# Row statistics of 35 tiles of the second layer norm: from VectorE to a router column and a ScalarE accumulator

## The reference, cut to what matters

```
xn = layernorm(x)
x  = x + graph_attention(xn, src, dst) + linear_attention(xn)
x  = x + experts(layernorm(x))

# in experts(x):
logits = x @ Wr + br                       # 256 -> 8
top_p, top_idx = top_k(softmax(logits), 2)
mu  = x.mean(-1);  var = ((x - mu)**2).mean(-1)
xn  = (x - mu) * rsqrt(var + 1e-5)
# each token goes through the FFNs (256 -> 1024 -> 256) of its two experts,
# weighted by the two renormalised probabilities
```

## Time and profile before

| | |
|---|---|
| median of three runs | 1897.31 us |
| profiled execution, first to last instruction | 1890.1 us |
| around it, against the median of the runs | 7.2 us |
| edge walk | some 95 to 1198 us |
| steps with late work | some 1012 to 1194 us |
| from the walk to the first FFN matmuls | to some 1285 us |
| mean granted TensorE clock | 0.937 |

### The profile page before, as it was taken

How to read it: one execution, slowest core, us unless ns; L and a number is a source line. 1 busy time by engine, 2 the same in 40 slices (tenths; PEclk the granted TensorE clock), 3 DMA queues, 4 the chain that set the end, 5 groups by cost and what they waited for, 6 DMA issues and landing times. The chain is left out here.

```text
span 1890.1 us, 46784 instructions
## 1 busy us (share of the span) xinstructions
PE 1581.7 (84%) x11358; PEld 1300.0 (69%) x11358; DVE 1368.5 (72%) x3833; ACT 1079.1 (57%) x3043; POOL 1218.3 (64%) x1135
## 2 busy tenths in 40 slices
PE   7858777788787989888887778629999999999995
PEld 5635555455566777777775666517888889888884
DVE  6656567677667888888888999897666656665662
ACT  4655566566666666677666776563444444444441
POOL 2077777777777777777677776105666666666663
PEclk8978899999999999999998888658999999999998
DMA  7745565566544555555555665652333333333332
GB/s 223 247 122 138 168 174 164 165 176 179 150 117 127 155 150 150 141 152 145 142 139 179 183 202 162 200 199 45 53 48 53 49 48 50 53 50 49 46 53 24
DMA packets 149158, 239.37 MB, mean 127 GB/s; under 512 B 27536, under 2 KB 114824, under 8 KB 147624
## 3 DMA queue, kind: packets, MB, share of 16 engines
q0 software_dynamic: 61216, 132.39, 30.4%
q1 hardware_dynamic: 85944, 103.15, 16.8%
q10 hardware_dynamic: 1744, 0.85, 0.2%
HBM read 180.78 MB, written 55.52 MB: 125 GB/s over the span
## 5 line engine op out<-in xcount | busy, mean ns | idle before, releaser
L843 POOL DMA_INDIRECT w_s<-table,w_s x784 | 806.4, 1029 | 279.9 <-issue 231.4
L2092 PE MATMUL bank<-w_s 128*128 128x260 f32 x1952 | 515.9, 410 | 110.3 <-DVE w_s L1536 110.0
L2092 PEld LDWEIGHTS bank<-w_s 128*128 128x128 f32 x1952 | 378.1, 201 | 206.0 <-DVE w_s L1536 139.9
L1026 ACT ACTIVATE w_s<-w_s 128x64 f32 x976 | 260.3, 337 | 68.3 <-ACT w_s L1021 68.1
L1536 DVE SCALAR_TENSOR_TENSOR w_s<-w_s 128x256 f32<-128x256 f32 x732 | 275.7, 426 | 26.7 <-ACT w_s L1026 18.9
L2294 PE MATMUL bank<-acc,w_s 128*128 128x256 f16 (+1 forms) x2736 | 290.4, 265 | 1.6 <-DVE acc L1937 1.5
L2315 PE MATMUL bank<-w_s,acc 128*128 x2520 | 284.5, 273 | 7.2 <-DVE acc L1951 5.5
L907 POOL DMA_INDIRECT out<-mid_g,low_g x105 | 177.2, 1687 | 151.2 <-ACT mid_g L1197 90.6
L2294 PEld LDWEIGHTS bank<-acc,w_s 128*128 x2736 | 252.9, 98 | 30.7 <-issue 2.1
L2315 PEld LDWEIGHTS bank<-w_s,acc 128*128 128x128 f16 x2520 | 245.8, 98 | 37.0 <-issue 8.7
L1033 ACT COPY w_s<-bank 128x512 bf16<-128x512 bf16 x244 | 142.1, 582 | 202.8 <-PE bank L2072 202.3
(11 more groups left out here) (308 smaller groups left out, 2187.6 us busy)
## 6 DMA issues: line engine op xcount, KB each, us to landing
stage<-in_L_ffn_W SPq DMA_DIRECT2D x32, 512.0 KB, 4.2
w_s<-table,w_s POOLq DMA_INDIRECT x784
w_s<-in_x SPq DMA_DIRECT2D x48, 256.0 KB, 4.0
w_s<-xT_d SPq DMA_DIRECT2D x96, 128.0 KB
w_park<-low_g SPq DMA_DIRECT2D x18, 512.0 KB
w_s<-w_park SPq DMA_DIRECT2D x9, 1024.0 KB, 9.1
xn_d<-acc SPq DMA_DIRECT2D x7, 896.0 KB, 5.0
table<-w_s SPq DMA_DIRECT2D x24, 260.0 KB, 3.5
```

What stands on the lines that cost most here:

```text
L843: pool.indirect_dma_start(out=ring[:, u, k, :], out_offset=None, in_=table[:, :], in_offset=bass.IndirectOffsetOnAxis(ap=srcT[:, (q * RING ...
L1026: last = act.activation(m[:, e, 0:GD], rows[:, e, 0:GD], ACT.Copy, scale=m[:, e, GD:HC])
L2092: last = pe.matmul(bank[2 + k.at % 2][:, 0:ROW], hot32[:, k.at % 4, s, :], msg[:, k.at % 2, s, :], start=s == 0, stop=s == SUB - 1)
```

## The change

Tiles 0 to 34 get their statistics in another way. The router matrix in the main memory gets a ninth column with the constant 1/256; it isn't centred, and the product with a raw row is that row's mean. ScalarE squares each of the 35 tiles (`act_square`, one tile per step, right behind `act_turn`) into a scratch tile of four slots, and its accumulator output gives the sum of squares per row. Behind the walk and `scale_group(6)`, VectorE makes means and variances of all 35 tiles with three small operations (`stats_rows`). The `bn_stats` and `bn_aggr` of these tiles go; those of the last two groups stay. The PSUM regions of the logits are 9 wide per tile, not 8, and their other readers and writers take the first 8 columns. The waits on `var3_ready` count from three instead of five groups. GpSimd's wait before a gather reads its register through a mask of 255.

```diff
-        wr_s = sb("wr_s", [P, KD, X])
+        wr_s = sb("wr_s", [P, KD, X + 1])
+        squares = beside_w1([P, T])
+        squared = beside_w1([P, 4, D])
...
-            return bank[(6, 2)[i]][:, 0:n * X].rearrange("p (t e) -> p t e", t=n)
+            return bank[(6, 2)[i]][:, 0:n * (X + 1)].rearrange("p (t e) -> p t e", t=n)
...
+            pool.memset(wr_s[:, :, X], 1.0 / D).then_inc(consts, 1)
...
-                        pool.wait_ge(msg_ready, pool.snap(free_r[u], min_val=1, max_val=J))
+                        pool.wait_ge(msg_ready, pool.snap(pool.snap(free_r[u], min_val=1, max_val=J) & 255).with_bounds(min_val=1, max_val=J))
...
+            def act_square(t):
+                act.wait_ge(x2_made, t // RG + 1)
+                if t >= 4:
+                    act.wait_ge(squares_made, t - 3)
+                act.activation(squared[:, t % 4, :], acc[:, t, 0:D], ACT.Square, accum_out=squares[:, t:t + 1]).then_inc(squares_made, 1)
...
                 if 0 <= n - FINAL - 6 < ADDED * RG:
                     act_turn(n - FINAL - 6)
+                    act_square(n - FINAL - 6)
...
-                act.wait_ge(var3_ready, STATS[n][1])
+                act.wait_ge(var3_ready, 3 + STATS[n][1] - ADDED)
...
+            def stats_rows(t1):
+                dve.wait_ge(squares_made, t1)
+                dve.wait_ge(logit_done, t1)
+                in_turn(dve, var3_ready, 0,
+                        lambda: dve.tensor_copy(mean_var[:, 0:t1, 0], logits(0)[:, :, X]),
+                        lambda: dve.tensor_tensor(mean_var[:, 0:t1, 1], mean_var[:, 0:t1, 0], mean_var[:, 0:t1, 0], ALU.mult),
+                        lambda: dve.scalar_tensor_tensor(mean_var[:, 0:t1, 1], squares[:, 0:t1], 1.0 / D, mean_var[:, 0:t1, 1], ALU.mult, ALU.subtract))
...
-                    if k == 5 and g < ADDED:
-                        stats_group(g)
...
             scale_group(GROUPS - 1)
+            stats_rows(ADDED * RG)
             stats_group(GROUPS - 2)
...
+                    pe.wait_ge(consts, 11)
```

More of the change, by code:

```diff
@@ L532, in build @@
         adds_ready, tau_turn = sem("adds_ready"), sem("tau_turn")
+        squares_made = sem("squares_made")
         rows_got = [sem(f"rows_got{u}") for u in range(2)]
@@ L608, in load_mix @@
                 elif n == 7:
-                    sp.dma_start(wr_s[:, :, :], wr.rearrange("(k p) n -> p k n", p=P)).then_inc(mix_in, 16)
+                    sp.dma_start(wr_s[:, :, 0:X], wr.rearrange("(k p) n -> p k n", p=P)).then_inc(mix_in, 16)
                 else:
@@ L1674, in wr_centred @@
                 for k in range(KD):
-                    dve.scalar_tensor_tensor(wr_s[:, k, :], bank[4][:, 0:X], -1.0 / D, wr_s[:, k, :], ALU.mult, ALU.add).then_inc(wr_ready, 1)
+                    dve.scalar_tensor_tensor(wr_s[:, k, 0:X], bank[4][:, 0:X], -1.0 / D, wr_s[:, k, 0:X], ALU.mult, ALU.add).then_inc(wr_ready, 1)
             def three(ap):
@@ L1699, in add_group @@
                 dve.scalar_tensor_tensor(z, z, 1.0, mid_of(g)[:, :, :], ALU.mult, ALU.add).then_inc(x2_made, 1)
+            def stats_rows(t1):
[5 more added lines that the diff above has]
+                        lambda: dve.scalar_tensor_tensor(mean_var[:, 0:t1, 1], squares[:, 0:t1], 1.0 / D, mean_var[:, 0:t1, 1], ALU.mult, ALU.subtract))
             def stats_group(g):
                 dve.wait_ge(x2_made, g + 1)
-                if g:
-                    dve.wait_ge(var3_ready, g)
+                dve.wait_ge(var3_ready, 3 + g - ADDED)
                 for k in range(RG):
@@ L1707, in stats_group @@
                 last.then_inc(stats_turn, 1)
-                dve.wait_ge(stats_turn, g + 1)
+                dve.wait_ge(stats_turn, g - ADDED + 1)
                 for k in range(RG):
@@ L1764, in pick @@
                 in_turn(dve, pick_turn, 15 * i,
-                        lambda: dve.tensor_tensor(lg, logits(i), wide1(root3[:, t0:t1]), ALU.mult),
+                        lambda: dve.tensor_tensor(lg, logits(i)[:, :, 0:X], wide1(root3[:, t0:t1]), ALU.mult),
                         lambda: dve.tensor_tensor(lg, lg, wide8(br_b[:, :]), ALU.add),
@@ L2208, in wr_sum @@
                 for k in range(KD):
-                    last = pe.matmul(bank[4][:, 0:X], ones[:, :], wr_s[:, k, :], start=k == 0, stop=k == KD - 1)
+                    last = pe.matmul(bank[4][:, 0:X], ones[:, :], wr_s[:, k, 0:X], start=k == 0, stop=k == KD - 1)
                 last.then_inc(wr_summed, 1)
```

## The result

Measured together on one chip, the kernel before took 1898.69 us (median of 5 runs, 1894.27 to 1901.55) and the changed one 1885.66 us (median of 5, 1885.35 to 1892.9): ratio 0.9954, 95% interval 0.9936 to 0.9973. By the ratio that is 8.7 us less (by its interval 5 to 12), by the two medians 13.0 us; the sum of the prediction had 8.6 us. The profiled execution took 1892.9 us with a span of 1891.0 us.

A forecast was written before the change was run, and what follows sets the result against it. VectorE's order of work was taken to pace the late walk. Span 1890.1 - 9.3 (walk) + 0.7 (tail) = 1881.5 us, plus 7.2 around it, gave 1888.7 us, 0.45% below the median; range 1879 to 1900 us.

The forecast's parts named there:

- VectorE paces the late walk and is where the return comes from: Late walk: VectorE busy 144.37 of 150 us, others wait for it; work taken off it early would be worth nothing.
- a sign that the prediction had named against itself: Early walk, 100 to 1000 us: the prediction is wrong if this part moves at all.
- VectorE loses 14.5 us in five groups: Late walk: removed statistics free 2.90 us of VectorE's queue per group, 5 x 2.90 = 14.5 us at most.
- The square at 0.45 us of ScalarE: Each tile's square on ScalarE costs 0.45 us, between 0.31 and 0.70, accumulator read-out free or 0.20 us.
- the rival of table changes: ScalarE in the walk: Square outside the exponential's set costs two loads per tile, 90 us; total 1964 us; chance 0.03.
- 9.3 us return in the walk: Late walk: four groups give 2.3 us each and one 0.1 us, together 9.3 us.
- ScalarE's coupling: Late-walk steps without extra VectorE work go by ScalarE's repeat, 3.3 us with squares; about 0.9 us lost per period.
- One group nearly empty: Late walk near 1161.48: slow TensorE sum delays the target matmuls, so removing statistics there gives 0.1 us, not 2.90.
- The tail pays 0.7 us: Behind the last scaling: three small VectorE operations on 35 columns add 0.7 us, 0.5 to 1.2.
- 7.2 us around the span: Outside the profiled span: median 1897.3 less span 1890.1 us, 7.2 us added to the forecast span.
- Waits for ScalarE of 5 us or more: Late walk: VectorE's waits for ScalarE's scaled copies grow from 1.1 us to 5 or more.
- the rival in which GpSimd sets the late pace: Late walk: GpSimd's gathers set the pace, a third of the return is left, 4 us net, 1893 us; chance 0.14.

## Why the prediction was right

1. *VectorE paces the late walk and is where the return comes from:* right. The early walk's waits for gathers are what they were (149.6 us, 77 times over the whole span, one of them late, against the earlier trace rows), and with the mask alone nothing moved. With the statistics gone the gain came with or without squares. The first scaling did come later, a sign that the prediction had named against itself; the profiles of both kinds overlap there, and it is not settled further.
2. *VectorE loses 14.5 us in five groups:* nearly. Its busy time in the five periods fell by 13.5 us. (All five statistics lie in the 150 us that the prediction shortened, so there it should have taken off 14.5 and not 4.6 x 2.90 = 13.4 us; the shares hardly change.)
3. *The square at 0.45 us of ScalarE, between 0.31 and 0.70, with or without a small companion, no table load:* right, 0.41 us with a companion of 190 ns, no load. That settles the rival of table changes.
4. *9.3 us return in the walk:* 8.7 us measured, over five periods and over the whole late walk alike. That this is so near is luck: single profiles scatter by 1.8 us in the five periods and more over the whole late walk, and the terms inside were wrong and made up for one another. The largest, 4 x 0.9 = 3.6 us for ScalarE's coupling, didn't exist: VectorE's waits for ScalarE's copies stayed at 0.8 us, and neither no squares nor two moved the five periods by more than that scatter. I had taken ScalarE's repeat of 2.91 us against VectorE's step of 2.60 for a limit; the squares went into ScalarE's own waiting for TensorE, which fell from 41.5 to 23.6 us. In its place stand 3.9 us of waits for TensorE, which the sum had charged with 2.8 - 1.2 = 1.6 us, and 1.5 us for GpSimd, which it had charged with nothing though it stood at 96%.
5. *One group nearly empty, because a slow sum holds the next target matmuls:* right in place and kind, too hard in size. TensorE, then VectorE, in the changed kernel, against the earlier trace rows:

```profile
1161.27 3.69 PE L2109 MATMUL bank<-w_s 128*128 128x260 f32 x8 [0.46 <-DVE w_s L1547]
...
1165.60 0.25 PE L2099 MATMUL bank<-w_s 128*128 x4
```
```profile
1163.72 0.22 DVE L1537 SCALAR_TENSOR_TENSOR w_s<-w_s 128x16 f32<-128x16 f32 x1
1165.89 0.26 DVE L1530 TENSOR_REDUCE w_s<-bank 128x32 f32<-128x96 f32 x1 [1.94 <-PE bank L2099]
```

   The sum still takes 3.69 us and VectorE now stands 1.94 us where its statistics stood. From 1163.72 to 1165.89 it is 2.17 us, against 3.05 before: 0.9 us came back, not 0.1.
6. *The granted clock at 0.85 or above:* right, 0.90. *Scaling to scaling from 32.5 to 30.5 us:* right in the fall. Over the four periods between the first five additions of embeddings it is 32.6 to 30.75 us; over the five between the first six scalings themselves 32.9 to 31.2.
7. *The tail pays 0.7 us:* right, 84.2 to 84.9. VectorE behind the last scaling:

```profile
1199.78 0.19 DVE L1716 COPY small<-bank 128x35 f32<-128x35 f32 x1
1200.01 0.20 DVE L1717 TENSOR_TENSOR small<-small 128x35 f32<-128x35 f32 x1
1200.24 0.20 DVE L1718 SCALAR_TENSOR_TENSOR small<-w_s,small 128x35 f32<-128x35 f32 x1
1200.54 2.38 DVE L1724 BATCH_NORM_STATS2 w_s<-acc 128x6 f32<-128x256 f32 x7
```

8. *7.2 us around the span:* wrong as a name. 1.9 us lie around the span; the other 5.3 us are the distance of one profiled execution from the median. Taken off a median the sum stands all the same: 8.6 predicted, 8.7 by the ratio; with an interval of 5 to 12 us and 13.0 by the medians, so close a match is chance.
9. *VectorE's busy share below 96%:* right, 90%. *Waits for ScalarE of 5 us or more:* wrong, the same error as in 4. The wait for gathered rows that was to prove the prediction wrong did appear, once, for 1.5 us: the rival in which GpSimd sets the late pace holds for that share.

## What to carry to other kernels

When the pacing engine gets lighter, don't price only the engine that receives the work: list every engine within a few per cent of the pace, for the return is cut by those. Cutting one of two limits side by side shows nothing, and looks like proof that neither counts; cut both. Read the size of a gain from a bounded stretch between two events of the paced part, since one execution's start of that part scatters by as much as the gain (8.7 us over ten profiles here). And profile one program twice before reading a difference of a few us: the bounded stretch itself scattered by 1.8 us.

## What the hardware showed that I had not expected

- Reading ScalarE's accumulator is an instruction of its own: 190 ns long, but 0.09 us of the queue.
- GpSimd's first tensor operation behind the last gather starts 9.7 to 10.8 us after that gather's end (twelve profiles), with nothing shown that it waits for (the earlier trace rows have 0.30 us between gathers). Held by a semaphore until VectorE's last message, it started 10.75 us after, at the end of the same range.
- While GpSimd adds 128x1792 elements (3.96 us), VectorE's messages and scalings, which read two operands from the main memory, don't get on until its end: 4.88 us for three messages of 1.09 us, 2.75 us for a scaling of 2.03 that began 0.87 us before the addition's end. A reciprocal (0.33 us) and the additions from PSUM (0.43 us) in that time took what they always take.
- Half of the adding matmuls left out brought TensorE's granted clock in the five periods from 0.90 to 0.64 (0.67 with fewer gathers too), nearer the lower of its two levels, 1.2 of 2.4 GHz; the walk got shorter all the same.
- The same program, with nothing changed, took 1896 us on some chips and 2310 us on one, and the sign of a 0.5% change wasn't the same on both.
